# FFN matrix product of token pairs 1 to 7 as seven Strassen block products instead of eight, in a fused attention, FFN and expert kernel

## What is computed

```python
x = x + _L0_xattn_ref(_layernorm(x, axis=-1), ctx_4096, ctx_4096)
x = x + _L0_ffn_ref(_layernorm(x, axis=-1), L0_ffn_W, L0_ffn_b, L0_ffn_A, L0_ffn_B, L0_ffn_gate_w, L0_ffn_gate_b)
x = x + _L1_xattn_ref(_layernorm(x, axis=-1), ctx_4096, L1_xattn_conv_w, L1_xattn_bn_gamma, L1_xattn_bn_beta)
x = x + _L1_ffn_ref(_layernorm(x, axis=-1), L1_ffn_router_weight, L1_ffn_router_bias, L1_ffn_expert_bias)

def _L0_ffn_ref(hidden_states, W, b, A, B, gate_w, gate_b):
    out = jnp.einsum('bsd,od->bso', hidden_states, W) + b        # W is 2048 x 2048
    scores = x @ gate_w.T + gate_b
    ...
    lora_outputs = jnp.stack([x @ A[:r, :].T @ B[:, :r].T for r in RANKS], axis=1)
    ...
    return out + final.reshape(bsz, seq, -1)
```

## Time and profile before

| | us |
|---|---|
| median of 3 runs (3251.45 to 3252.09) | 3251.5 |
| span of the profiled execution | 3248.4 |
| pair 0, from PE's first FFN matmul to pair 1's first | 206.7 |
| pairs 1 to 6, each | 190.5 to 191.1 |
| pair 7 | 190.9 |
| after the last FFN matmul | 422.8 |

### The profile page before, as it was taken

One profiled execution on the slowest core, in us unless ns is written; L12 is line 12 of the kernel. 1 busy time (PEld: TensorE's weight loads), 2 busy tenths in 40 slices (PEclk: granted clock), 3 DMA queues, 4 the chain that ended last, 5 costly groups with the idle time before them and its releaser, 6 DMA issues. The chain is left out here.

```text
span 3248.4 us, 46726 instructions
## 1 busy us (share of the span) xinstructions
PE 2953.1 (91%) x12946; PEld 1590.3 (49%) x12946; DVE 2740.0 (84%) x7152; ACT 2257.7 (70%) x5939; POOL 1580.1 (49%) x1161
## 2 busy tenths in 40 slices
PE   5999999999999996999999999999999999838886
PEld 3666666666666664444444444444444444412322
DVE  4999999999999996676887979788796978778996
ACT  6878888888887862665675857667585765468773
POOL 5889989989999993001212112121211212005776
PEclk8999999999999998999999999999999999959997
DMA  5555555555555545254564737456473744453664
GB/s 187 175 180 158 164 176 165 157 175 173 157 168 180 159 121 178 76 163 124 172 163 135 223 93 204 146 161 177 131 213 104 203 149 128 110 201 143 244 249 167
DMA packets 272039, 532.17 MB, mean 164 GB/s; under 512 B 32664, under 2 KB 132760, under 8 KB 248992
## 3 DMA queue, kind: packets, MB, share of 16 engines
q1 hardware_dynamic: 245600, 422.17, 41.8%
q10 hardware_dynamic: 15168, 71.34, 7.6%
q0 software_dynamic: 11008, 35.66, 3.3%
HBM read 401.07 MB, written 128.02 MB: 163 GB/s over the span
## 5 line engine op out<-in xcount | busy, mean ns | idle before, releaser
L1055 PE MATMUL acc<-xh,wq 128*128 128x512 f16 x4096 | 1203.4, 380 | 44.8 <-DMA wq<-w_split 16.1
L1055 PE MATMUL acc<-xl,wq 128*128 128x512 f16 x2048 | 757.6, 379 | 0.0
L1283 ACT ACTIVATE unused<-c_first,minus_guess 128x256 bf16<-128x256 f32 x1024 | 505.2, 494 | 281.9 <-DVE minus_guess L1591 221.4
L1055 PEld LDWEIGHTS acc<-xh,wq 128*128 128x128 f16 x4096 | 399.6, 98 | 529.6 <-DVE x_first L1717 21.5
L984 POOL DMA_DIRECT2D c_first<-ctx_pairs x120 | 66.6, 556 | 857.9 <-DVE mk L1642 847.6
L1055 PEld LDWEIGHTS acc<-xl,wq 128*128 128x128 f16 x2048 | 200.6, 98 | 242.5 <-issue 1.4
L439 PEld LDWEIGHTS bu<-m_iz,zf 128*128 128x128 f32 x2048 | 278.9, 191 | 50.3 <-issue 35.6
L439 PE MATMUL bu<-m_iz,zf 128*128 128x128 f32 (+2 forms) x2048 | 293.0, 301 | 5.5 <-DVE zf L640 5.5
L458 PE MATMUL bx<-m_ic,pf 128*128 128x256 f32 x1024 | 241.5, 390 | 35.8 <-POOL pf L343 35.8
L458 PEld LDWEIGHTS bx<-m_ic,pf 128*128 128x128 f32 x1024 | 193.1, 194 | 72.1 <-POOL pf L343 47.5
L1265 ACT ACTIVATE unread<-cf 128x256 bf16<-128x256 f32 x256 | 106.1, 415 | 129.3 <-DVE feat_pair L1690 97.3
(11 more groups left out here) (355 smaller groups left out, 7054.1 us busy)
## 6 DMA issues: line engine op xcount, KB each, us to landing
wq<-w_split SPq DMA_DIRECT2D x512, 256.0 KB, 3.2
c_first<-ctx SPq DMA_DIRECT2D x64, 512.0 KB, 6.7
xt<-xT SPq DMA_DIRECT2D x64, 512.0 KB, 6.4
x_pairs<-xo SPq DMA_DIRECT2D x64, 512.0 KB, 3.3
c_first<-ctx_pairs POOLq DMA_DIRECT2D x128, 256.0 KB, 4.9
x<-xn_pairs SPq DMA_DIRECT2D x32, 1024.0 KB, 5.4
out_pairs<-ost SPq DMA_DIRECT2D x32, 1024.0 KB, 5.0
x_first<-x SPq DMA_DIRECT2D x15, 2048.0 KB, 7.7
```

Of the source, the lines that this page charges most:

```text
L1055: return pe.matmul(acc[b][:], ws[(WQ * o + k // CK) % WR][:, k % CK, a, :], x[:, k, :], start=start, stop=False)
L1283: act.activation(signs[:, u // 2, t] if n == COUNTS - 1 else unused[u % 2][:], ct[k % CR][:, t], ACT.Sign, bias=guess[q % 2][:, u:u + 1], ...
```

## The change

For pairs 1 to 7 the 2048 x 2048 by 2048 x 512 product is cut in halves along output, input and tokens, and made as seven products of half the size in each direction (Strassen, Winograd's form) instead of eight.

- **PE.** `times(i, x, u)` makes product `x` (0 to 6) in four parts `u`, each two output tiles of 256 tokens in one PSUM bank: 48 matmuls with 256 columns (2 tiles x 8 `k` x 3 cross products), so 28 parts hold 1344 matmuls a pair. Four of the seven products get corrections, 80 matmuls of 256 columns in all. `gates` is now 16 fp32 matmuls straight from `xr`, and the next pair's is made at the end of the pair before, so pair 0 holds two and pair 7 none.
- **Weights.** Three products use blocks of `w_split`; four use sums of blocks, `w_joined`, which are made **during pair 0** in 16 chunks: ACT loads 1 MB of fp32 weights into one of two staging buffers (`load_stage`), POOL adds (`join`, four 128x512 additions), ACT writes the high fp16 parts (`joined_high`, four ACTIVATE of 128x512), DVE the low parts (`joined_low`, four), and ACT stores the chunk (`prepare`, 1 MB in pieces of 512 bytes). The fp16 chunk has a single buffer, `w_parts`: before the high parts of chunk c are written, ACT waits until the store of chunk c-1 has landed (`joined_out`). A pair now needs 112 weight pieces of 256 KB instead of 64, through the same ring of eight.
- **x.** POOL makes four differences of x's blocks (`t_sum`), ACT and POOL or DVE split each of the seven operands in high and low fp16 (`high`, `low_of`).
- **Eviction.** POOL multiplies x by the deviation beforehand (`scale_x`, `scale_all`); DVE then adds or subtracts a PSUM bank in one operation (`evict`, 28 of 128x512 a pair; in pair 0 `take`, one instead of two). Bias goes into the corrections. The squares' sums move from DVE to POOL.
- **Masks** go through DRAM: written in quarters by POOL's queue, read back in quarters by ACT's.

The diff, cut to its core:

```diff
+def times(i, x, u):                                   # PE, pairs 1 to 7
+    pe.wait_ge(x2_ok, evicted(i, BANKS * x + u) - BANKS + 1)
+    for o in (2 * u, 2 * u + 1):
+        bank = acc[u][:, HT * (o % 2):HT * (o % 2 + 1)]
+        for k in range(HK):
+            if k % CK == 0:
+                at = loaded(i, CHUNKS * x + 2 * o + k // CK)
+                pe.wait_ge(w_in[at % WR], 16 * (at // WR + 1))
...
+            for a, b in ((0, 0), (1, 0), (0, 1)):
+                mm = pe.matmul(bank, ws[at % WR][:, k % CK, a, :], part(q, b)[:, k, :], ...)
...
 def gates(i):
-    for k in range(KT):
-        for x, g in ((xh, gh), (xh, gl), (xl, gh)):
-            mm = pe.matmul(ps_g[0:GC, :], g[:, k, :], x[:, k, :], ...)
+    for k in range(KT):
+        mm = pe.matmul(ps_g[0:GC, :], g32[:, k, :], xr[i % 2][:, k, :], start=k == 0, stop=k == KT - 1)
...
+CHUNKS_AT = {0: (0,), 1: (1,), 2: (2,), 3: (3, 4), 4: (5,), 5: (6,), 6: (7, 8), 7: (9,), 8: (10,), 9: (11, 12), 10: (13,), 11: (14,), 12: (15,)}
+TAKES_AT = {1: (1,), 2: (2,), 3: (3,), 4: (4,), 5: (5,), 7: (6,), 8: (7,), 9: (8,), 11: (9,), 12: (10,), 14: (11,), 15: (12,)}
...
+def prepare(c):                                       # ACT
+    act.wait_ge(joined_lo, 4 * c)
+    j, g = (c - 1) // 2, (c - 1) % 2
+    act.dma_start(w_joined[g, :, :, j, :, :].rearrange("s p a n -> p s (a n)"), w_parts.rearrange("p s a n -> p s (a n)")).then_inc(joined_out, 16)
+    if c + 1 < CHUNKS:
+        load_stage(c + 1)
+def joined_high(c):                                   # ACT
+    if c == 0:
+        act.wait_ge(b_rows_in, 48)
+    else:
+        prepare(c)
+        act.wait_ge(joined_out, 16 * c)
+    for m, n in enumerate((S1, S3, S2, S4)):
+        act.wait_ge(join_ok, 4 * c + m + 1)
+        act.activation(w_parts[:, OG * n:OG * (n + 1), 0, :], stage[c % 2][:, n, :]..., ACT.Copy, scale=W_SCALE).then_inc(joined_hi, 1)
+def joined_low(c):                                    # DVE
+    for m, n in enumerate((S1, S3, S2, S4)):
+        dve.wait_ge(joined_hi, 4 * c + m + 1)
+        dve.scalar_tensor_tensor(w_parts[:, OG * n:OG * (n + 1), 1, :], stage[c % 2][:, n, :]..., W_SCALE, ..., ALU.mult, ALU.subtract).then_inc(joined_lo, 1)
+def join(c):                                          # POOL
+    a11, a21, a12, a22 = [stage[c % 2][:, n, :] for n in range(4)]
+    pool.wait_ge(stage_in[c % 2], 32 * (c // 2 + 1))
+    pool.tensor_tensor(a22, a22, a21, ALU.add).then_inc(join_ok, 1)
...
 def step(i, s, u, o):                                 # ACT
+    if i == 0:
+        for c in CHUNKS_AT.get(o, ())[:1]:
+            joined_high(c)
...
+    if not is_last(i) and o == (10 if i else 14):
+        high(i + 1, 1 - s, B11, 0)
+        high(i + 1, 1 - s, B11, 1)
     for im, _, _, om in masked[:1]:
         mask_first(im, om)
...
 def step(i, s, u, o):                                 # DVE
     for im, sm, um, om in masked[:1]:
         mask_step(im, sm, um, om)
+    if i == 0:
+        for c in CHUNKS_AT.get(o, ())[:1]:
+            joined_low(c)
...
     for im, sm, um, om in masked[:1]:
         mask_second(im, om)
...
 def evict(i, n):                                      # DVE, for the two operations of take
+    dve.wait_ge(*product_done(i, x, u))
+    dve.wait_ge(xs_ok, ...)
+    dve.tensor_tensor(xq, xq, acc[u][:].rearrange("p (k t) -> p k t", k=2), op).then_inc(x2_ok, 1)
```

More of the change, by code:

```diff
@@ L1022, in pair @@
             def pair(i, s, u):
                 for o in range(OT):
[L1024 to L1030 removed]
+                    if o == 0 and i == 1:
+                        second_opens()
+                    elif o == 0:
+                        opens(i, s)
@@ L1032, in _ @@
+            first_pair()
+            for i in range(1, NPAIR):
+                pair(i, i % 2, i // 2)
+            pool.wait_ge(m_out, 16 * NGRP * NPAIR)
         @block.tensor
@@ L1194, in tail, with first_pair @@
-            def tail(i, s, u):
-                pe.wait_ge(bad_ok, 2 * NPAIR)
-                pe.wait_ge(arhs_ok, 2 * NPAIR)
-                pe.matmul(ps_g[0:1, 0:1], ones[:, 0:1], bad[:], start=True, stop=True).then_inc(flag_mm, 1)
-                last_stats3()
-                rows3_(i)
-            pairs(pe, pair, tail)
+            def first_pair():
+                main(0)
+                setup()
+                main(1)
+                gates(0)
+                main(2, {8: lambda: tokens(0)})
+                main(3, {4: lambda: rows_std(0), 8: lambda: low_rows(0), 14: lambda: correct(0)})
+                for o in (1, 2, 3):
+                    correct(o)
+                for o in range(4, OT):
+                    main(o, {4: lambda: tokens(1)} if o == OT - 1 else {})
+                    correct(o)
+                    if o == OT - 3:
+                        gates(1)
@@ new lines, in pair @@
+            def pair(i):
+                after = {(0, 0): lambda: rows_std(i), (0, 3): lambda: low_rows(i)}
+                after |= {(1, 2): lambda: stats3(i), (2, 0): lambda: rows3_(i)} if i == 1 else {(0, 2): lambda: stats3(i), (1, 1): lambda: rows3_(i)}
+                if not is_last(i):
+                    after |= {(6, 0): lambda: gates(i + 1), (6, 2): lambda: tokens(i + 1)}
+                for x in range(NP):
+                    for u in range(BANKS):
+                        times(i, x, u)
+                        if (x, u) in after:
+                            after[x, u]()
@@ L1202, in _ @@
+            first_pair()
+            for i in range(1, NPAIR):
+                pair(i)
+            pe.wait_ge(bad_ok, 2 * NPAIR)
+            pe.wait_ge(arhs_ok, corrected(NPAIR))
+            pe.matmul(ps_g[0:1, 0:1], ones[:, 0:1], bad[:], start=True, stop=True).then_inc(flag_mm, 1)
+            last_stats3()
+            rows3_(NPAIR)
         @block.scalar
@@ L1736, in step @@
                 masked = mask_steps(i, s, u, o)
-                if not first(i):
-                    trail(i, 1 - s, u, o)
+                norm_at = min(NORM3_1 if i == 1 else NORM3)
+                evicts = EVICTS_AT.get(o, ()) if i else ()
+                if o == 0 and i == 1:
+                    for last in TAKES_LATE:
+                        take(last)
+                    low_of(1, 1, A, 1)
+                    low_of(1, 1, N3, 1)
+                elif o == 0 and i:
+                    evict(i - 1, NEV - 1)
@@ L1764, in step @@
+                if i and o == norm_at - 1:
+                    variance3(i)
+                if o == 15 and not is_last(i):
+                    variance2(i + 1)
                 for im, sm, um, om in masked[1:]:
```

866 lines of the change are left out of this document (579 added, 287 removed).

## The result

The changed kernel takes 3717.1 us (3715.6 to 3719.4), the kernel before 3251.5 in the same runs: ratio 1.1435, 95% interval 1.1419 to 1.1452. It is slower, as forecast, but by 466 us and not by 92, outside the range and away from what every rival gave. The profiled execution has a span of 3714.3 us.

A forecast was written before the change was run, and what follows sets the result against it. PE's own pace was taken to bound the kernel. To the profiled 3248.4 us came +153.3 (pair 0), -39.7 (pairs 1 to 6), -21.6 (pair 7) and 3.1 from profile to median: 3343.5, range 3240 to 3430.

The forecast's parts named there:

- What bounds the kernel now: Kernel before: PE's own pace sets pairs 1 to 7, busy 187.5 of 190.5 us in pair 3.
- Pairs 1 to 7 on PE: Main matmuls -19.2 us, corrections +1.8, gates +3.4, weight loads hidden: 177.1 us a pair with PE alone.
- Weights: Pairs 1 to 7: gaps in the weights' stream starve PE 7 us a pair, bounds 0 and 15, making 184.1.
- one hole that costs 5.5 us: Once a pair, some 13 us without weights during ACT's transfers, of which the ring covers 7.5.
- Rival C: Pairs 1 to 7 bound by the weights' stream, some 195 to 202 us each, 3421 at the lower end; chance 0.10.
- Who hides the rest: Other engines in a pair: DVE about 143 us, ACT 137, POOL about 109; none reaches PE's 177.
- Pair 0: Joining puts a serial chain on ACT, 9.7 us for each of 15 chunks; the pair takes 360.0 us, +153.3.
- B: Faster: in pair 0 joining lies beside counts and picks, PE's gain comes through, 3207 or 3158 us; chance 0.15.
- D: Pairs 1 to 7: weight load not hidden behind 256 columns, 278 us a pair, near 4170; chance 0.02.

The follow-up runs named there:

- PE lightened: Kernel before with two of three cross products, the one of the low part of x left out for tiles 1 to 15: 3200.1 us.
- POOL light: Changed kernel with POOL's differences, scalings, low parts and first folding of squares cut to 8 elements each: 3415.9 us.
- the fills: Changed kernel with POOL's differences, scalings, low parts and first folding of squares replaced by fills of about the same length that read nothing from SBUF: 3577.8 us.
- Mended order and second buffer: Changed kernel with context loads at position 2, in pair 0 also ahead of the joining, and a second buffer for the joined chunk: 3623.9 us.

## Why the prediction was wrong

The 373 us between the forecast and the result lie in pairs 1 to 6 (304), in pair 0 (51.5) and in pair 7 (18).

**What bounds the kernel now.** "PE's own pace sets these pairs" was right and said too little. DVE's 155.7 us of 190.5 looked like 35 us of room, but a pair fell only by 6 of them, to 184.4 us, with PE lightened. In that run DVE and ACT wait for each other (count, then guess, then count). The step that failed first is that a busy time was read as an engine's need.

**Pairs 1 to 7 on PE.** The terms held. A matmul of 256 columns took 0.109 us, the weight loads were hidden, the gates took 13.9 us for 13.8, and with POOL light PE was busy 177.9 us of a pair for which 177.1 was predicted. (By its own terms that number is 190.7 - 14.0 = 176.7.) The clock was the term that was missing: while PE stood from 2374 to 2399 us its mean granted clock was 0.58, some of it at 1.2 GHz, and the next 48 matmuls took 2408.80 - 2401.79 = 7.0 us instead of 5.2. Over pair 3 the clock is 0.90 and PE busy 184.2; with POOL light it is 0.98. So the low clock is a consequence of the waits, not their cause. Pair 7 took 187.0 us for 169.3. It shares their cause: it is 16.5 us shorter with the fills and 22.7 with POOL light.

**Weights.** 7 us a pair were predicted; PE waited 6.8 for joined pieces in pair 3. The size is right, the mechanism only in part: instead of one hole that costs 5.5 us there are six waits, the longest 3.4, and without joined pieces PE still waited 6.1. Rival C (pairs above 190 because weights are late) had the length on its side and the wrong mechanism.

**Who hides the rest.** This is the step that cost most: pairs 2 to 6 took 231.6 us and not 184.1, 47 more each. ACT came out at 135.8 (137 predicted) and POOL at 110.3 (109); DVE at 164.7 for 143, of which the hold on its feature instructions alone is 29.4 - 12.9 = 16.5. "None reaches 177" compared each engine's sum with the pair. It missed that POOL's instructions hold up DVE's, which the trace of before shows (0.61 and 0.63 us for what takes 0.42), that POOL issues the context tiles behind its new work, and that a chain with 6 us of slack was given differences, high parts and low parts in the middle. The runs put 18, 12 and 13 us on these; the 5 that are left of the 47 are there with POOL light too.

**Pair 0.** The serial chain was the right mechanism: 154 us for the joining, 145.5 predicted. Its largest term was too long: the store landed in 5.7 us in the median, not in 7.0 (transfers of the changed kernel in pair 0: queue, count, size, median us to landing).

```profile
w_joined<-x_parts ACTq DMA_DIRECT2D x16, 1024.0 KB, 5.7
```

The Trainium skill's fit ("DMA: Bandwidth & Descriptors", Anatomy of one DMA) gives an estimate of 4.4 for it; the row decides. Where nothing else stands between two chunks, it is 8.9 us from one's first high part to the next one's (1601.37 to 1610.26), not 9.7; that is 15 x 0.8 = 12 us counted too much. And yet pair 0 came out 51.5 longer than 360. Most of that isn't the joining's: without it pair 0 took 257.5 us, 43 more than the 360.0 - 145.5 = 214.5 of the sum. The waits of ACT, DVE and POOL in pair 0 show one of the missing terms:

```profile
ACT x_parts L1530 <- DMA w_joined<-x_parts: 123.4, 15, 12.8
ACT slope L1712 <- DVE st L1987: 35.0, 4, 13.8
```
```profile
DVE st L1987 <- DMA c_first<-ctx_pairs: 44.1, 12, 10.9
```
```profile
POOL t_sums L1118 <- DMA t_sums<-wT: 126.4, 7, 53.4
POOL spare L1118 <- DMA spare<-wT: 92.0, 7, 16.0
```

ACT has its 15 waits for the store, as forecast. They are 8.2 us each and not 5 to 7, because they begin before the store is issued, while DVE's last low part is still to come. But DVE waits 44.1 us for context tiles, which are issued by POOL behind a joining that waits for the staging loads (POOL and then DVE in order of time):

```profile
1392.66 1.26 POOL L1118 TENSOR_TENSOR t_sums<-t_sums 128x512 f32<-128x512 f32 x1 [12.28 <-DMA t_sums<-wT]
...
1397.88 1.11 POOL L1103 DMA_DIRECT2D c_first<-ctx_pairs  x2
```
```profile
1401.68 0.48 DVE L1987 BATCH_NORM_STATS2 st<-c_first 128x6 f32<-128x128 f32 x2 [8.43 <-DMA c_first<-ctx_pairs]
```

Starts in the trace, set beside the sum's own steps, say where the time went:

- The first high part came at 1365.9 instead of 1356.5: 9.4.
- The last chunk's came at 1637.4 instead of 1608.9: 19.1 more. Steps 1, 4 and 8, in which a group of context tiles begins, are 19.4 longer; the rest cancels.
- The take that lets tile 15 start came at 1671.7 instead of 1632.4: 10.8 more. Step 12, where a group begins too, lies here.
- From there to pair 1 it was 22.4 us instead of 11.3: 11.1 more. 3.7 of it is a wait for the next pair's gates, which ACT copies only after the counts of step 14, and 5.4 is the clock. PE had waited 11.8 us and had a granted clock of 0.50 from 1672 to 1678, 1.2 GHz; tile 15's 12 and 36 matmuls took 5.3 and 10.4 us instead of 2.6 and 7.8 (PE in order of time):

```profile
1672.41 5.30 PE L1318 MATMUL acc<-x_parts,wq 128*128 128x512 f16 x12 [11.77 <-DVE x_first L2123]
1681.42 0.44 PE L1409 MATMUL ps_t<-ident,gates_sb 70*128 70x70 f32 x4 [3.71 <-ACT gates_sb L1568]
...
1683.24 10.59 PE L1318 MATMUL acc<-x_parts,wq 128*128 128x512 f16 x36
```

These make 50.4, and the pair began 1.1 us sooner than in the kernel before. Only the context tiles have a run behind them: asked for early, they took 21 us off, and no staging loads, behind which they stand, took 35. Mended order and second buffer brought little (38 together). The chain may then run over ACT's own issues of staging loads (3.3 us for two) and POOL's additions; that was not tried, and how much each of these has of the rest stays open.

**The rivals.** B (the gain comes through) was far off: pair 0 grew by 205 us, and pairs 1 to 6 had no gain to let through. D is out by the spacing; its price was also too low, since 278 us for 146.5 are 132 a pair and not 118. No rival said that the pairs get longer for a cause other than weights, and the range ended at 3430 for this reason.

## What to carry to other kernels

Before a change that makes the busiest engine faster is costed, take work off that engine in the kernel as it is: here one run showed that 52 us less on PE a pair are worth 6. Work that goes to GpSimd isn't free for VectorE: count every DVE instruction with two SBUF inputs that may meet it, keep GpSimd's instructions short, and put nothing that waits ahead of loads in the queue that issues them. A chain that passes between engines has the slack that a run shows, not the one that busy shares show.
